# A four-layer gated cross-attention kernel: leaving out TensorE's products of constants

## The reference, cut to what matters

```
x = x + tanh(g_xattn[0]) * L0_xattn(layernorm(x), ctx, ...)   # A0: 16-head softmax attention
x = x + tanh(g_ffn[0])   * L0_ffn(layernorm(x), ...)          # M0: 8 experts, top 2, plus 2 shared
x = x + tanh(g_xattn[1]) * L1_xattn(layernorm(x), ctx, ...)   # A1: 16-head softmax attention
x = x + tanh(g_ffn[1])   * L1_ffn(layernorm(x), ...)          # SW: attention with switched value and output experts
x = x + tanh(g_xattn[2]) * L2_xattn(layernorm(x), ctx, ...)   # ML: mLSTM in parallel form, 4 heads
x = x + tanh(g_ffn[2])   * L2_ffn(layernorm(x), ...)          # CF: quantized linear, width-3 convolution, SiLU, linear
x = x + tanh(g_xattn[3]) * L3_xattn(layernorm(x), ctx, ...)   # WA: one wide head, two norms, an FFN of 512
x = x + tanh(g_ffn[3])   * L3_ffn(layernorm(x), ...)          # M3: 16 experts in 4 groups, top 4, plus shared
```

## Time and profile before

| | |
|---|---|
| time, median of 3 runs | 2598.35 us |
| the profiled execution's own time | 2615.43 us |
| its span, first to last instruction | 2613.4 us |
| TensorE (PE) busy | 2329.8 us, 89%, 19938 matmuls |
| VectorE (DVE) busy | 1580.6 us, 60% |
| ScalarE (ACT) busy | 1411.8 us, 54% |
| GpSimd (POOL) busy | 143.7 us, 5% |
| DMA | 115.19 MB, mean 44 GB/s |
| mean granted TensorE clock | 0.979 of 2.4 GHz |

### The profile page before, as it was taken

The page is one execution under the profiler, slowest core; times in us unless marked ns, Lnnn a source line. Parts: engine busy times, 40 slices in busy tenths (PEclk is TensorE's granted clock), DMA queues, the critical chain, the costliest instruction groups (busy, mean ns, idle before and its releaser), DMA issues.

```text
span 2613.4 us, 51527 instructions
## 1 busy us (share of the span) xinstructions
PE 2329.8 (89%) x19938; PEld 1626.1 (62%) x19938; DVE 1580.6 (60%) x5307; ACT 1411.8 (54%) x3970; POOL 143.7 (5%) x180
## 2 busy tenths in 40 slices
PE   5999889998899888999899998998989989899887
PEld 2668556675566755667556775567755676565765
DVE  3754666547666376664756647556475565755656
ACT  4376264753647436475365744557345573455734
POOL 0000100001000010000100001000100001000010
PEclk9999999999999899999999999999999999999999
DMA  3024000340004300043000420005200051000510
GB/s 156 1 66 114 9 13 1 80 99 17 5 1 100 80 15 7 1 100 80 17 5 1 111 69 17 5 1 122 58 17 5 1 138 42 19 3 9 137 35 5
DMA packets 312292, 115.19 MB, mean 44 GB/s; under 512 B 268737, under 2 KB 295361, under 8 KB 311793
## 3 DMA queue, kind: packets, MB, share of 16 engines
q1 hardware_dynamic: 312048, 111.90, 17.0%
HBM read 63.64 MB, written 48.23 MB: 43 GB/s over the span
## 4 chain that ended last, share of the span: by engine, by line
PE 52%; DVE 24%; ACT 9%; DMA 7%; issue 4%; POOL 3%; SPq 1%; DVEq 0%; ACTq 0%
PE banks L462 5%; PE banks L406 5%; PE banks L343 5%; ACT PP L820 3%; PE banks L292 3%; DVE nm L1163 2%; PE banks L546 2%; POOL mv L1682 2%; PE banks L340 2%; PE banks L430 2%; PE banks L573 2%; PE banks L679 2%; DMA mix_d<-gs 2%; PE banks L354 2%; DMA o_d<-oa 2%
## 5 line engine op out<-in xcount | busy, mean ns | idle before, releaser
L820 ACT ACTIVATE PP<-banks,nm 128x128 f32<-128x128 f32 x1568 | 450.3, 397 | 171.6 <-DVE nm L1163 117.4
L1163 DVE TENSOR_REDUCE nm<-banks 128x4 f32<-128x512 f32 (+1 forms) x400 | 260.0, 675 | 309.3 <-PE banks L343 263.7
L406 PE MATMUL banks<-w_sb,PP 128*128 128x128 f32 x1536 | 248.2, 285 | 44.4 <-ACT PP L827 24.5
L827 ACT ACTIVATE PP<-banks 128x512 f32<-128x512 f32 (+1 forms) x400 | 242.2, 613 | 63.2 <-PE banks L406 48.3
L292 PE MATMUL banks<-identb 128*128 128x256 bf16 x1632 | 267.4, 288 | 7.2 <-ACT PP L978 4.5
L406 PEld LDWEIGHTS banks<-w_sb,PP 128*128 128x128 f32 x1536 | 166.4, 142 | 138.4 <-ACT PP L827 90.9
L1682 POOL TENSOR_TENSOR mv<-mv,half 128x2 f32<-128x2 f32 x160 | 115.5, 722 | 2278.9 <-DVE mv L1060 2278.9
L292 PEld LDWEIGHTS banks<-identb 128*128 128x128 bf16 x1632 | 161.0, 104 | 68.0 <-issue 26.4
L462 PE MATMUL banks<-w_sb,qk 128*128 128x128 f32 x1280 | 193.4, 287 | 1.3 <-DVE qk L1298 1.3
L462 PEld LDWEIGHTS banks<-w_sb,qk 128*128 128x128 f32 x1280 | 162.9, 191 | 30.3 <-issue 11.4
L811 ACT ACTIVATE xnT<-banks 128x256 f32<-128x256 f32 x128 | 48.8, 381 | 191.0 <-PE banks L300 191.0
(11 more groups left out here) (281 smaller groups left out, 4329.0 us busy)
## 6 DMA issues: line engine op xcount, KB each, us to landing
va<-v_d SPq DMA_DIRECT2D x32, 512.0 KB, 4.1
o_d<-oa SPq DMA_DIRECT2D x64, 256.0 KB, 3.9
va<-o_d SPq DMA_DIRECT2D x32, 512.0 KB, 4.1
pv_d<-PP SPq DMA_DIRECT2D x32, 256.0 KB, 2.1
oa<-pv_d SPq DMA_DIRECT2D x32, 256.0 KB, 3.6
v_d<-PP SPq DMA_DIRECT2D x16, 512.0 KB, 4.6
v_d<-tmp SPq DMA_DIRECT2D x16, 512.0 KB, 5.6
w_sb<-weights SPq DMA_DIRECT2D x1, 5603.0 KB, 23.1
```

Of the source, the lines that this page charges most:

```text
L406: e = pe.transpose(bank(k, 2)[:, cols(j)], P[k][:, 512 * (u % 2) + 128 * j:][:, 0:128], ident)
L820: e = act.activation(P[k][:, 512 * (u % 2) + 128 * j:][:, 0:128], bank_[:, cols(j)], ACT.Exp, bias=nm[k][:, m:m + 1])
L827: act.activation(PT[k][:, 512 * (u % 2):512 * (u % 2) + maps * 128], bank(k, 2)[:, 0:maps * 128], ACT.Copy).then_inc(pT_ok[k], 1)
L1163: e = dve.tensor_reduce(m, b3(scores[:, 0:maps * 128], maps), AX.X, ALU.max, negate=True)
```

## The change

The list `SPARES` becomes 101 zeros. `spare` is still called in the same places when the program is built, and issues nothing. All waits, all other instructions, the order on each engine and all due times stay.

```diff
-SPARES = (
-    0, 0, 1, 0, 0, 0, 2, 0, 0, 0, 1, 0, 0, 0, 0, 3, 0, 6, 0, 0, 6, 4, 0, 0, 0, 0, 3, 0, 0, 0, 0, 0, 4, 0, 0, 0, 2, 0, 0, 0,
-    0, 4, 0, 4, 0, 0, 2, 0, 0, 0, 0, 0, 0, 0, 0, 0, 0, 0, 0, 2, 2, 0, 0, 0, 0, 0, 0, 0, 0, 7, 1, 0, 0, 0, 0, 0, 15, 0, 6, 4,
-    0, 0, 10, 0, 2, 1, 0, 0, 0, 2, 3, 0, 0, 2, 0, 0, 0, 0, 3, 0, 0,)
+SPARES = (0,) * 101
```

## The result

The changed kernel took 2696.8 us (median of 4 runs, 2680.7 to 2716.0), the kernel before 2598.0 us (the three runs above and a fourth): ratio 1.038, 95% interval 1.034 to 1.041. Slower was right; +31 us was forecast and +99 us came. The time is inside the wide range only by 3 us and far outside the forecast's own range of 2610 to 2660 us.

A forecast was written before the change was run, and what follows sets the result against it. TensorE, busy 89% of the span, was taken as nearest to the bound; 52 us back from the chain and 83 us lost to the lower clock gave +31 us, 2629 us against the median; 8-in-10 range 2572 to 2700 us.

The forecast's parts named there:

- the wide range: Whole kernel: the time expected in 8 of 10 cases, 2572 to 2700 us.
- The products' time on the chain, 52 us back, bounds 0 and 68: Constant products on the chain that ended last: three quarters of their 68 us there comes back at an unchanged clock.
- The price of the lower level, 0.44 us per us: TensorE work at 1.2 GHz: each us spent there loses 0.44 us, a little under line 679's 0.49.
- The Trainium skill's half: Whole kernel: the skill's rule of one minus the clock ratio prices 190 us more at 1.2 GHz at 95 us.
- ML, CF and SW's end, 8.7 us per turn: Both lanes' work there: half of the 17.3 us per turn not already paid is lost to the lower clock.
- One fall per turn where the 6 and 4 products stand: In front of lines 388 and 395: 3.4 us per turn at the lower level, costing 1.7 us.
- Nothing anywhere else: Outside ML, CF, SW's end and one fall at lines 388 and 395: no further loss; the rest costs nothing.
- the 190 us: Whole kernel: extra time at 1.2 GHz, about 190 us for 83 us lost, making 300 us in all.
- rival 3: Attention: a quarter of its 85 us per turn also falls to 1.2 GHz, 75 us more, 2704 us; chance 0.20.
- line 343 at double its time: Attention: this line taking twice as long would show the forecast wrong.
- Rival 1: Whole kernel: clock holds, mean above 0.956, and the chain shortens; 2546 us when complete; chance 0.13.
- Rival 2: Whole kernel: 46 us lost to the lower clock cancels 52 us coming back, 2592 us; chance 0.18.

The follow-up runs named there:

- one_row: Kernel before with all 1632 constant products kept, each using one row and one column of the identity in place of 128 by 128: 2759.6 us, ratio 1.061.
- no_wa: Kernel before without the 11 constant products per lane and turn of WA, M3 and the start of A0: 2626.9 us, ratio 1.009.
- wa_only: Changed kernel with only the 11 constant products per lane and turn of WA, M3 and A0's start put back: 2665.2 us, 1.023 of the kernel before.
- no_mlcf: Kernel before without the 38 constant products per lane and turn of ML and CF: 2645.4 us, ratio 1.017.
- no_att: Kernel before without the 41 constant products per lane and turn of attention stages A0 and A1: 2602.4 us, ratio 1.002.

## Why the prediction was wrong

By its own steps:

- *The products' time on the chain, 52 us back, bounds 0 and 68.* Right in size. one_row against the change gives 63 us, give or take 13 and up to 20 too much (above), at the lower clock, where a product takes longer. A rougher way agrees: cut the two profiled executions into cells of 10 us, and a line through them gives 48 us back at an unchanged clock (32 us with cells of 20 us).
- *The price of the lower level, 0.44 us per us.* Right, if a little high. 99 + 63 = 162 us for 458 - 62 = 396 us more is 0.41, and with 48 us for the products' time it is 0.37; the line through the cells gives 0.39. Stretches differ: A1's long falls cost 0.42 (7.1 of 17.1 us). The Trainium skill's half (TensorE: Matmul & The Clock Gate, section Terms) would be 198 us for the same time, an estimate from that page; the runs show less.
- *ML, CF and SW's end, 8.7 us per turn.* Right. ML and CF stand at 0.70 in the turn shown, forecast 0.65; with SW there are 17.9 + 2.6 = 20.5 us per turn more at the lower level, at 0.41 us per us 8.4 us. After what the products give back, 3.7 and 0.9 us are left of it.
- *One fall per turn where the 6 and 4 products stand.* That place is the end of A0 and not of A1, as I called it. A0 has 3.4 us per turn more (0.4 to 3.8), which is the 3.4 that the step had. In part this is luck: only three of the eight turns fell there, for 6.8 to 10.2 us.
- *Nothing anywhere else.* This is the step that failed, "I add one fall per turn" as the whole of what lies outside ML, CF and SW's end, and with it the 190 us. WA and M3 have 13.0 us per turn at the lower level and A1 9.8 us, 22.8 of the 46.7 us more that the table adds up to. No term had them. Net of what the products give back these three stretches lost 3.3 + 2.6 + 1.5 = 7.4 us per turn, 59 us in eight, most of the 68 us by which the forecast was short. WA was missing altogether, though its entries stood in the list: 2 to 3 products each looked too few to matter, and no_wa and wa_only show 25 to 32 us for them.

Of the rivals, 3 named attention and a time of 2704 us, close to the measured one, but by its mechanism only in part: A1 fell, A0 hardly, and WA, which it did not name, cost as much. That its time came close is luck. (Its two stretches were 93% busy, not 91: 45.92 + 32.91 of 85 us.) The sign of being wrong that the prediction named, line 343 at double its time, is what A1 shows (L340, 2.08 us against 1.13). Rival 1 is refuted by the mean clock of 0.915. Rival 2 had the loss and the time that comes back cancel; leaving out the products of ML and CF alone costs 45 us net (no_mlcf). The Trainium skill's rule on which rival 3 leaned (TensorE: Matmul & The Clock Gate, Part 4: PE-mode transpose) is not borne out: with transposes as fillers the clock is 0.986.

Why a fall in A1 lasts 17 us is not settled. TensorE shows almost no gap in that time by the profile, and one_row shows that a busy TensorE is not enough; many of the products there have 32 rows (L340) or 32 columns (L351). Whether the thin products are what keeps the clock down was not tried: a kernel with fillers of 32 rows was not run, and which turns fall in A1 stays open, too.

## What to carry to other kernels

When fillers are taken out or placed, go through every place where they stand, the small ones first, and ask what the clock did in the stretch before; a stretch at 1.00 is no sign that its fillers do nothing. Price the time at the lower level from pairs of rows of the same work (here 0.4 us per us), and the fillers' own time by a filler that takes the same time and holds no clock. A filler in the gap of a wait is nearly free (0.02 us each in A0 and A1); one more behind it costs most of its length (0.08 to 0.09 of 0.11 us). A kernel that comes out even may have lost to the clock what it won in time (no_att).

## What the hardware showed that was not expected

- Products of one row and one column, 256 columns streamed, do nothing for the clock here: 0.913 with 1632 of them, 0.915 without any. Products of 128 rows and 32 columns hold it at 0.988, as do bf16 transposes at 0.986. Whether one_row fails by its rows or by its single column was not told apart.
- The clock stayed at 1.2 GHz for 17 us in which the profile shows TensorE busy almost without a gap, in four of eight turns behind the same gap of 1.50 us.
- Eleven products per lane and turn, 176 in the kernel and 19 us of TensorE's time, are worth 25 to 32 us.
